# Mamba-2 layer with low-rank MLP in fp32: one gating instruction per chunk instead of four, and the W_out loads on GpSimd's DMA queue

## What is computed

```python
normed = layer_norm(x, gamma, beta)
z, xs, Bm, Cm, dt = split(normed @ W_in + b_in)   # 2048, 2048, 64, 64, 8
dt = softplus(dt + dt_bias); decay = exp(dt * -exp(A_log))
# per step t: h = decay*h + (dt*xs) B^T ;  y = h C
y = (y + D_skip * xs) * silu(z)                    # the gating
x = _layernorm(x + (x + y @ W_out + b_out))        # W_out: the output projection
x = _layernorm(x + gelu(x @ U1 @ V1 + b1) @ U2 @ V2 + b2)
```

## Time and profile before

| | us |
|---|---|
| median of 2 timed runs (7988.75, 8299.06) | 8143.91 |
| the profiled execution's own time | 8043.64 |
| its span, core 2, the slowest | 8042.1 |
| spans of the 8 cores | 7898.9 to 8042.1 |
| TensorE busy in the span | 6714.6 (83%) |
| VectorE, ScalarE, GpSimd busy | 1251.8, 814.2, 749.2 |
| DMA moved | 861.71 MB, mean 107 GB/s |

### The profile page before, as it was taken

One profiled execution on the slowest core, in us unless ns is written; L12 is line 12 of the kernel. 1 busy time (PEld: TensorE's weight loads), 2 busy tenths in 40 slices (PEclk: granted clock), 3 DMA queues, 4 the chain that ended last, 5 costly groups with the idle time before them and its releaser, 6 DMA issues.

```text
span 8042.1 us, 59511 instructions; the slowest of 8 cores (7898.9 to 8042.1 us)
## 1 busy us (share of the span) xinstructions
PE 6714.6 (83%) x19875; PEld 4116.7 (51%) x19875; DVE 1251.8 (16%) x3053; ACT 814.2 (10%) x1410; POOL 749.2 (9%) x1412
## 2 busy tenths in 40 slices
PE   7788887888878888788897888978888788897898
PEld 5364553645535455364553645546455464553655
DVE  1112011110111102111111111111111111111111
ACT  1011010100101001010110101101011010110101
POOL 0020100201002010020100101001010010100101
PEclk9778777788777877788887878778778787676777
DMA  4424324243232432424333243332433324233232
GB/s 140 130 62 131 119 92 131 67 132 115 89 131 74 146 94 90 132 75 144 100 107 114 75 139 100 108 115 76 136 100 120 109 80 136 90 105 110 71 120 81
DMA packets 214646, 861.71 MB, mean 107 GB/s; under 512 B 37067, under 2 KB 37963, under 8 KB 181453
## 3 DMA queue, kind: packets, MB, share of 16 engines
q1 hardware_dynamic: 122190, 572.59, 21.6%
q0 software_dynamic: 92160, 285.30, 11.8%
HBM read 840.71 MB, written 16.78 MB: 107 GB/s over the span
## 4 chain that ended last, share of the span: by engine, by line
PE 71%; DMA 12%; DVE 8%; issue 4%; ACT 2%; DVEq 2%; ACTq 0%; POOL 0%; SPq 0%; POOLq 0%
PE PS L627 11%; PE PS L526 11%; DMA woB<-wo 7%; PE PS L561 6%; PE PS L487 5%; PE PS L492 5%; PE PS L752 4%; PE PS L736 3%; PE PS L708 2%; PE PS L595 2%; PE PS L591 2%; PE PS L704 2%; PE PS L740 2%; PE PS L509 2%; DMA v1B<-v 2%
## 5 line engine op out<-in xcount | busy, mean ns | idle before, releaser
L561 PE MATMUL PS<-woB,x1tm 128*128 128x512 f32 x2048 | 977.9, 618 | 161.2 <-DMA woB<-wo 159.4
L627 PE MATMUL PS<-uT,wzB 128*128 128x256 f32 x4096 | 1024.8, 414 | 0.0
L526 PE MATMUL PS<-wxB,uT 128*128 128x512 f32 x2048 | 982.5, 644 | 7.2 <-DMA wxB<-wx 6.9
L627 PEld LDWEIGHTS PS<-uT,wzB 128*128 128x128 f32 x4096 | 847.2, 209 | 166.0 <-issue 32.7
L561 PEld LDWEIGHTS PS<-woB,x1tm 128*128 128x128 f32 x2048 | 370.6, 193 | 753.9 <-issue 752.6
L526 PEld LDWEIGHTS PS<-wxB,uT 128*128 128x128 f32 x2048 | 419.5, 206 | 549.9 <-issue 548.1
L314 PE MATMUL PS<-identR,statT 128*1 128x128 f32 x96 | 35.6, 371 | 635.8 <-DVE statT L309 608.6
L752 PE MATMUL PS<-Hs,u2B 128*128 128x256 f32 x2048 | 549.4, 394 | 10.7 <-ACT Hs L744 10.7
L245 POOL DMA_DIRECT2D u1B<-u x128 | 68.8, 538 | 4401.5 <-PE PS L721 4322.7
L487 PE MATMUL PS<-MTT,xsT 128*128 128x128 f32 x1024 | 405.4, 500 | 81.8 <-DVE xsT L540 81.8
L752 PEld LDWEIGHTS PS<-Hs,u2B 128*128 128x128 f32 x2048 | 402.8, 198 | 80.3 <-issue 22.2
(11 more groups left out here) (122 smaller groups left out, 5475.7 us busy)
## 6 DMA issues: line engine op xcount, KB each, us to landing
wxB<-wx SPq DMA_DIRECT2D x256, 1024.0 KB, 5.4
woB<-wo SPq DMA_DIRECT2D x512, 512.0 KB, 4.5
wzB<-wz POOLq DMA_DIRECT2D x256, 512.0 KB, 3.8
v1B<-v POOLq DMA_DIRECT2D x512, 128.0 KB, 2.4
u2B<-u POOLq DMA_DIRECT2D x512, 128.0 KB, 2.3
u1B<-u POOLq DMA_DIRECT2D x128, 128.0 KB, 2.3
xT<-x SPq DMA_DIRECT2D x16, 1024.0 KB, 5.4
out<-rT SPq DMA_DIRECT2D x32, 512.0 KB, 2.6
```

Of the source, the lines that this page charges most:

```text
L526: pe(lambda e, k=k, c=c, n4=n4, buf=buf: e.matmul(ps(2048 + n4 * 512, 512), uT[:, k, c * 128:(c + 1) * 128], wxB[:, buf, n4 * 512:(n4 + 1) ...
L561: pe(lambda e, k=k, n2=n2, buf=buf: e.matmul(ps(1024 + n2 * 512, 512), gT_slice(k), woB[:, buf, n2 * 512:(n2 + 1) * 512], start=(k == 0), ...
L627: pe(lambda e, ft=ft, k=k, buf=buf, bank=bank: e.matmul(ps(bank * 512, 256), wzB[:, buf, k, :], uT[:, k, :], start=(k == 0), stop=(k == 7) ...
```

## The change

Two edits. The gating of a chunk, four VectorE multiplications of 128x512 with one PSUM bank each, becomes one of 128x2048 over all four banks; it writes the same values to the same places of x1tm. And the loads of W_out, the first three and the 32 per tile behind the output projection's steps, are issued by GpSimd instead of SyncE. The lines below L499 move up by two: L509 becomes L507, L561 becomes L559.

```diff
--- before.py
+++ after.py
@@ -346,7 +346,7 @@
     for i in range(3):
         dma("gpsimd", wzB[:, i], wz_hbm(i), dWZ[i])
         dma("sync", wxB[:, i], wx_hbm(i), dWX[i])
-        dma("sync", woB[:, i], wo_hbm(i), dWO[i])
+        dma("gpsimd", woB[:, i], wo_hbm(i), dWO[i])
         dma("gpsimd", v1B[:, i], v1_hbm(i), dV1[i])
         dma("gpsimd", u2B[:, i], u2_hbm(i), dU2[i])
     dma("gpsimd", u1B[:, 0], u1_hbm(0), dU1[0])
@@ -495,14 +495,12 @@
                    rd=[hS, MTvT], wr=[ps(off, 128)])
 
     def gating(c):
-        for i4 in range(4):
-            ve(lambda e, c=c, i4=i4: e.tensor_tensor(
-                x1tmT[:, i4 // 2,
-                      (i4 % 2) * 512:(i4 % 2) * 512 + 512].rearrange(
-                          "p (a b) -> p a b", a=4),
-                ps(2048 + i4 * 512, 512).rearrange("p (a b) -> p a b", a=4),
-                szT[:, i4 * 4:(i4 + 1) * 4, c * 128:(c + 1) * 128], ALU.mult),
-               rd=[ps(2048 + i4 * 512, 512), szT], wr=[x1tmT])
+        gflat = x1tmT[:].rearrange("p a b -> p (a b)")
+        ve(lambda e, c=c, gflat=gflat: e.tensor_tensor(
+            gflat.rearrange("p (a b) -> p a b", a=16),
+            ps(2048, 2048).rearrange("p (a b) -> p a b", a=16),
+            szT[:, :, c * 128:(c + 1) * 128], ALU.mult),
+           rd=[ps(2048, 2048), szT], wr=[x1tmT])
 
     def hinc_mms(c):
         for h in range(HEADS):
@@ -565,7 +563,7 @@
                    rd=[x1tmT, woB[:, buf]], wr=[ps(1024 + n2 * 512, 512)])
             nxt = 32 * j + 16 * c + k + 4
             if nxt <= 32 * n_tiles:
-                dma("sync", woB[:, buf], wo_hbm((nxt - 1) % 16),
+                dma("gpsimd", woB[:, buf], wo_hbm((nxt - 1) % 16),
                     dWO[(nxt - 1) % 3])
         for n2 in range(2):
             pe(lambda e, n2=n2: e.matmul(
```

## The result

The changed kernel is slower. The ratio to the kernel before, run beside it on the same chip, is 1.0198, with a 95% interval of 1.0150 to 1.0245. That is clear of no change, while it stays open whether it is more or less than 2%. Its median over 11 executions is 8312.35 us (8162.85 to 8562.86); that of the kernel before, over 10, is 8214.8 us (7988.75 to 8407.23). The medians take in executions in which the cores of a die ran longer at a lower granted clock; the ratios here leave those out, and where a profile had four such cores (e1, e6), its stage times are the mean of the other four. So the medians stand closer together (1.2%) than the ratio says, and the ratio decides.

The account below looks back on a forecast made before the run. TensorE, busy 83% of the span, was taken as the bound, the output projection hanging on woB load latency. 8043.6 + 82 (gating) + 10 (clock) + 67 (queue) = 8202.6, say 8200 us; own range 8150 to 8250, full range 8090 to 8320.

Parts of the forecast that it names:

- The gating: State increment: its first matmul waits for the one merged multiplication, 32 times 2.56 us, 82 us in all.
- The clock behind it: State increment: after the stand-still the granted clock may rise at another moment, -13 to +36 us, 10 us taken.
- The queue's term: Output projection: woB loads from GpSimd come later, five refills one behind the other per chunk; 67 us after discounts.
- x: Output projection: how much later a woB load comes on GpSimd's queue, taken as 0.6 us, costing 160x in all.
- two corrections only: Output projection: four low-clock chunks of 32 left out (84 us), then a fifth off for less queueing (67 us).
- 160 x 0.6 = 96 us: Output projection: the queue's cost with every delay on the path, the end of its range for equal queueing.
- The other queues: GpSimd's and SyncE's other loads, and the start: no later load blocked, wzB pushed back harmlessly; nothing added.
- How the numbers follow: Whole kernel: no-change line at 2%, 161 us, or 8204; chances slower 0.48, within 2% 0.49, faster 0.03.
- A: Output projection, rival: GpSimd's loads land in 3.8 us even three at a time; 8101 us; chance 20%.
- B: Output projection, rival: software loads queue worse, delay 1.2 us per load, 192 us, time 8328; chance 22%.
- C: Whole kernel, rival: more idle time keeps the clock up at the end, some 50 us back, 8150; chance 8%.
- What would show it: Changed profile: gating 2290 ns x32, L507 wait about 82 us, woB waits some 220 us or more, landing 4.5 to 4.7.

Follow-up runs that it names:

- e1: The kernel before with the merged gating alone, woB loads still on SyncE; ratio 1.0118 (1.0021 to 1.0216).
- e6: The kernel before with four woB buffers instead of three and woB loads on GpSimd; no ratio, lowest of 8 executions 7881.05 us, median 8240.36.
- e3: The kernel before with two gating multiplications of 128x1024, two PSUM banks each, woB loads on SyncE; ratio 1.0051 (0.9985 to 1.0117).
- e12: The changed kernel run once more, unaltered; no ratio, its lowest execution 8095.29 us against 7942.14 for the kernel before beside it.
- e2: The kernel before with the woB loads on GpSimd alone, four gating multiplications kept; ratio 1.0128 (1.0069 to 1.0187).
- e5: The kernel before with four woB buffers instead of three, loads on SyncE; ratio 0.9744 (0.9692 to 0.9796).
- e4: The kernel before with every second woB refill on GpSimd, the others on SyncE; ratio 1.0117 (1.0045 to 1.0188).
- e8: The kernel before with the loads of U1, V1 and U2 on SyncE instead of GpSimd; ratio 0.9759 (0.9663 to 0.9855).

## Why the prediction was right and where it was wrong

**The gating (82 us): right.** 32 waits of 2.59 us, 82.9 us in all; the stage grew by 85.2. The 2 us over are 0.07 a chunk: before, the increment started at 4193.90, slightly ahead of the modelled end of the last y matmul (4193.17 + 0.79). Length 2292 ns, as said from the xsT copy. e3 shows the mechanism was the right one: without the dependency of the first matmul the cost is zero.

**The clock behind it (10 us, between -13 and +36): right in sign and size.** The increment took 8.3 us more in the changed kernel and 4.1 more in e1 and e12, against a profile of the kernel before that was the highest of its kind. The three profiles with the merged gating have 176.1, 176.1 and 180.3 us, the seven with four multiplications or two 163.3 to 172.0, and the means differ by 11 us. The granted clock of the stage is 0.63 to 0.65 in the first and 0.67 to 0.70 in the others.

**The queue's term (67 us): mis-sized.** The mechanism, a loop of latency with five turns on the path, is confirmed by e2, e5 and e6. x came out at 0.58 where 0.6 was taken. What failed are the two discounts, the "two corrections only". "The 4 chunks of two tiles fall out of the 32" was read from one chunk of one core; the last four lose 2.84 us each. And "a fifth off", for loads that queue less when issued further apart, had no row for its size, and no run shows it: with all of woB on GpSimd the median landing was 4.6 to 4.9 us, never below the 4.5 of before. The undiminished 160 x 0.6 = 96 us, written there as an end of the range, was the value: 92.5 in e2, 93.7 and 95.6 in the changed kernel.

**"The other queues", put at nothing: wrong, by -17 to -21 us.** U1 lost 18, the start 5, the MLP won 40 to 43. At the start the prediction looked at the wrong load: a later wzB shows nowhere, but the woB loads, which now go out first, came with a later landing of the constants (last section). U1 and the MLP it had no step for; it followed the order of GpSimd's issues and took each to begin as soon as its buffer was free. These errors are opposite in sign to the discounts' and nearly cancel them: 67 was foretold for the queue in all; 76 came in e2 and 73 in the changed kernel.

**The sum and the number.** 82 + 10 + 67 = 159 us was foretold, 85 + 8 + 94 + 18 + 5 - 43 = 167 came in the first six lines of the table; the forecast's ratio of 1.019 stands against 1.0198. That it fits so well is in good part luck: the discounts took 27 us too much off, and 21 us came back in stages that were put at nothing. The 8200 us itself was on the scale of one execution of 8043.6. The median of the changed kernel's executions came 112 us above it because of the scale: the kernel before, too, has a median of 8214.8 with more executions, 171 above the 8043.6 from which the sum was made.

**The step that failed** where the sum was turned into slower or not is in "How the numbers follow": "2% of 8043.6 is 161 us, about what a measurement can tell from no change here", and with it the split of the likeliest case, 26 above and 24 below. What the comparison of the two kernels could tell was 0.5% to either side, so the likeliest case, 1.9% slower, lay wholly among the changes that can be told from none. By the forecast's own range of 8150 to 8250 it should have counted as slower, and not half as no change. The sum was sound to 8 us in 159, though two of its terms were not; the statement made of it was wrong.

**The rivals.** A is refuted by e4 and by 4.6 to 4.7 us of landing in e2 and after, B by the same and by x = 0.58. C (the clock gives some 50 us back) is not shown: the mean clock by core was 0.784 to 0.801 before and 0.788 to 0.797 after. It varied as much between executions of one kernel, so 50 us either way could not be seen, and it stays open. "What would show it" was met throughout: 2292 ns x32, a wait of 82.9 us in 32 times, a woB wait over 220 us, landing between 4.5 and 4.7, clock 1.00 in 96% of the chunks.

## What to carry to other kernels

A merged read of several PSUM banks costs its whole length if the next writer needs the first of them at once, and cost nothing here when the first two banks were let go early; look for a wait of the same shape in the trace and take its price. For a ring of buffers write down the loop (work, release, issue, landing), divide by the number of buffers and compare with the step: where the loop is longer, half a microsecond of issue counts once per turn, and one more buffer can be worth more than the choice of queue (here 190 us against 92). Take nothing off a bound without a row that says so, and when a queue gets other work, compare all stages that use it, the unedited ones too.

## What the runs showed that I had not expected

**GpSimd begins an issue late once per tile, and the place moves with its sequence.** In the kernel before, GpSimd's issues in the MLP have one gap per tile while the buffer has long been free:

```profile
3937.27 0.54 POOL L245 DMA_DIRECT2D u2B<-u  x1 [0.83 <-PE PS L752]
3937.80 0.54 POOL L245 DMA_DIRECT2D v1B<-v  x1
3941.29 0.54 POOL L245 DMA_DIRECT2D u2B<-u  x1 [2.96 <-PE PS L736]
```

TensorE then stands still for a v1B load, in a stage where most of these do not make it wait:

```profile
3944.36 0.67 PE L736 MATMUL PS<-PT,v1B 128*128 128x256 f32 x2 [1.86 <-DMA v1B<-v]
```

In e2, where 32 more issues per tile go through GpSimd, the late issue stands at the second load of U1 instead, first GpSimd and then TensorE:

```profile
3924.77 0.54 POOL L245 DMA_DIRECT2D u1B<-u  x1 [35.69 <-PE PS L721]
3927.84 0.54 POOL L245 DMA_DIRECT2D u1B<-u  x1 [2.52 <-PE PS L721]
```

```profile
3927.13 1.10 PE L721 MATMUL PS<-uT,u1B 128*128 128x256 f32 x4 [1.33 <-DMA u1B<-u]
3930.34 3.75 PE L721 MATMUL PS<-uT,u1B 128*128 128x256 f32 x8 [2.12 <-DMA u1B<-u]
```

Counted along GpSimd's DMAs from the first as no. 1, it is always the same position. In the kernel before, e1 and e3 it is no. 227, 315, 403 and so on, every 88 (the number of its DMAs in a tile), 2.7 us late. In e4 it is every 104, 1.9 us late; in e2, e6 and the changed kernel every 120, 2.0 us late. With 104 and 120 there is a second, shorter one in each tile, at a woB load (1.25 us) or a wzB load (1.4 us). It does not follow the time, and in e8, with only the wz loads left on GpSimd, it showed twice in the whole run.

That the late issue costs TensorE the time is borne out within the runs. In e2 it falls into U1 in the tiles 1 to 14 (counted from 0) and not in the first and the last: U1 took 20.2 us there, and 18.5 and 19.3 in these two. In e4, where half of woB is on GpSimd too but the late issue stays in the MLP, the MLP took 1050.7 us, against 1051.5 to 1060.9 in the kernel before, e1, e3 and e5, which send nothing new to GpSimd. So it is the place of the late issue and not the added loads. It accounts for the -40 and +18 us as to place and rough size: 2.5 us per tile taken out of the MLP, 1.2 put into U1. Of the -40, 21 are shorter waits for v1B (53.0 and 31.9 us, each on its slowest core); the granted clock of the MLP rose with it, from 0.96 to 0.98. Why GpSimd is late there stays open; no run here was made to settle it.

**The start hangs on when the constants land.** ScalarE's first instruction waits until all the small constants that SyncE loads have landed, and the whole first tile waits behind it. In the kernel before:

```profile
11.19 0.73 SPq L245 DMA_DIRECT2D onesR<-onesc  x1
14.30 0.94 SPq L245 DMA_DIRECT2D woB<-wo  x1
ACT L355 <- DMA onesR<-onesc: 21.3, 1, 21.3
```

And in the changed kernel:

```profile
2.23 0.53 POOL L245 DMA_DIRECT2D woB<-wo  x1
9.78 0.44 SPq L245 DMA_DIRECT2D onesR<-onesc  x1
ACT L355 <- DMA onesR<-onesc: 26.7, 1, 26.7
```

The last constant is issued no later, yet it lands 5 us later, since three woB loads of 512 KB that used to stand behind it on SyncE now go out ahead of it on GpSimd. The other runs go the same way: with a fourth such load (e6) the wait ends at 29.7 us, and with the loads of U1, V1 and U2 moved behind the constants (e8) at 18.6.

**Waits cost twice.** In e8 the shorter waits came with faster matmuls (592 to 494 ns in U1), and behind the merged gating with slower ones (520 to 551 ns in the increment in the changed kernel, e1 and e12, against 494 to 508 in the others looked at). The granted clock went with it, as a mean over all such stages from 0.64 to 0.83 in U1 and from 0.67 to 0.63 in the increment. What a wait costs in these stages is more than its own length.
